# A chain of attention and feed-forward layers on one core: layer norm statistics taken pair by pair, and two norms merged

## What is computed

```python
def _layernorm(x, axis=-1, eps=1e-05):
    m = jnp.mean(x, axis=axis, keepdims=True)
    v = jnp.var(x, axis=axis, keepdims=True)
    return (x - m) / jnp.sqrt(v + eps)

x = x + _L0_xattn_ref(_layernorm(x), ctx_512, ...)            # cross attention, 16 heads, 1500 keys
x = x + _L0_ffn_ref(_layernorm(x), ...)                       # 8 experts, the best 2
x = x + _L1_xattn_ref(_layernorm(x), ctx_512, ...)
x = x + _L1_ffn_ref(_layernorm(x), L1_ffn_rhs)                # int8 product
x = x + _L2_xattn_ref(_layernorm(x), ctx_512, ctx_512, ...)
x = x + _L2_ffn_ref(_layernorm(x), ...)                       # product in the frequency domain
x = x + _L3_xattn_ref(_layernorm(x), ctx_512, ...)            # two attentions with MLPs
x = x + _L3_ffn_ref(_layernorm(x), ...)                       # routed blocks
```

```python
x = _ln(xx, ln1_g, ln1_b)
x = x + _mha(x, x, a1...)      # causal self attention, then MLP
x = _ln(x, ln2_g, ln2_b)
return x + _mha(x, ee, a2...)  # cross attention, then MLP
```

## Time and profile before

| | |
|---|---|
| median of 3 runs | 4266.44 us |
| profiled execution | 4266.73 us |
| its span | 4264.9 us |
| busy, share of the span: PE, DVE, ACT, POOL | 91%, 80%, 65%, 64% |
| L146 `bn_stats` | 224, median 0.276 us each |
| L149 `bn_aggr` | 224, median 0.149 us each |
| L155 subtract and multiply | 224, median 0.34 us each |
| L162 power, on POOL | 28, median 1.65 us each |

### The profile page before, as it was taken

How to read it: one execution, slowest core, us unless ns; L and a number is a source line. 1 busy time by engine, 2 the same in 40 slices (tenths; PEclk the granted TensorE clock), 3 DMA queues, 4 the chain that set the end, 5 groups by cost and what they waited for, 6 DMA issues and landing times. The chain is left out here.

```text
span 4264.9 us, 103800 instructions
## 1 busy us (share of the span) xinstructions
PE 3879.5 (91%) x40555; PEld 2833.5 (66%) x40555; DVE 3391.7 (80%) x6723; ACT 2768.2 (65%) x5364; POOL 2709.2 (64%) x2473
## 2 busy tenths in 40 slices
PE   6999999978887999999889999996897799999986
PEld 4777777755554777777657777775676477777765
DVE  7999998768778888888688888886754788888863
ACT  5777777644545777777567777773442577777752
POOL 3887888756764777777647676775000377767761
PEclk9999999979998999999889999998898799999988
DMA  4333333124432111111011111110000111111100
GB/s 113 96 90 96 89 95 96 32 63 131 122 109 69 47 44 50 44 50 47 10 49 52 42 47 46 48 47 20 3 1 17 44 50 44 50 44 47 47 17 15
DMA packets 112883, 236.97 MB, mean 56 GB/s; under 512 B 14984, under 2 KB 53016, under 8 KB 111016
## 3 DMA queue, kind: packets, MB, share of 16 engines
q1 hardware_dynamic: 111944, 230.27, 18.9%
q10 hardware_dynamic: 448, 0.06, 0.0%
HBM read 165.10 MB, written 50.26 MB: 50 GB/s over the span
## 5 line engine op out<-in xcount | busy, mean ns | idle before, releaser
L520 POOL TENSOR_TENSOR wst<-wst 125x384 bf16<-125x384 f32 (+1 forms) x1536 | 1635.3, 1065 | 801.3 <-ACT wst L724 735.0
L724 ACT ACTIVATE wst<-ps 125x448 f32<-125x448 f32 x3072 | 1499.0, 543 | 406.8 <-PE ps L166 397.6
L781 DVE TENSOR_TENSOR wst<-wst 125x512 bf16<-125x512 f32 (+1 forms) x1536 | 1395.7, 909 | 255.0 <-ACT wst L724 246.5
L166 PE MATMUL ps<-big,cx 128*125 128x448 bf16 (+1 forms) x6144 | 1436.3, 355 | 0.0
L166 PEld LDWEIGHTS ps<-cx,wst 125*128 125x128 bf16 x23040 | 1105.7, 98 | 355.4 <-issue 60.5
L166 PE MATMUL ps<-cx,wst 125*128 125x65 bf16 (+2 forms) x23040 | 1202.8, 204 | 28.4 <-POOL wst L520 14.3
L166 PEld LDWEIGHTS ps<-big,cx 128*125 128x125 bf16 (+1 forms) x6144 | 814.9, 137 | 271.6 <-ACT wst L724 8.9
L166 PE MATMUL ps<-cx,big 128*128 128x500 bf16 (+1 forms) x2688 | 714.0, 319 | 28.2 <-DVE wst L751 14.5
L748 DVE CUSTOM_DVE_ANT_0 wst<-ps,wst 128x500 bf16<-128x500 f32 x896 | 603.2, 673 | 162.2 <-PE ps L166 122.9
L673 ACT ACTIVATE wst<-ps 128x500 bf16<-128x500 f32 x896 | 531.0, 593 | 231.5 <-PE ps L166 187.6
L751 DVE TENSOR_REDUCE wst<-ps 128x1 f32<-128x500 f32 x896 | 600.0, 670 | 34.0 <-PE ps L166 26.7
(11 more groups left out here) (240 smaller groups left out, 4101.9 us busy)
## 6 DMA issues: line engine op xcount, KB each, us to landing
cx<-ctxT SPq DMA_DIRECT2D x96, 375.0 KB, 3.5
cx<-ctxN SPq DMA_DIRECT2D x64, 377.9 KB
cx<-in_ctxN SPq DMA_DIRECT2D x64, 375.0 KB
cx<-ctxT SPq DMA_DIRECT2D x96, 187.5 KB, 3.8
ctxN<-cx SPq DMA_DIRECT2D x32, 377.9 KB
ynN<-cx SPq DMA_DIRECT2D x32, 377.9 KB
cx<-ynN SPq DMA_DIRECT2D x32, 377.9 KB
cTs<-in_ctxT SPq DMA_DIRECT2D x64, 187.5 KB, 6.8
```

Of the source, the lines that this page charges most:

```text
L166: return t.matmul(o, l, r, start=start, stop=stop, skip_group_check=True)
L520: g.tensor_tensor(pl[r][0:KP, at:], pf[r][0:KP, at:], pf[r][0:KP, at:].bitcast(BF16)[:, 1::2], ALU.subtract).then_inc(s["plp"], 1)
L724: e.activation(pf[T % 3][0:KP, cols], bank(2 + n2 % 3, 448)[0:KP], ACT.Exp, scale=scale).then_inc(s["ev"], 1)
L781: v.tensor_tensor(pl[r][0:KP, 0:to], pf[r][0:KP, 0:to], pf[r][0:KP, 0:to].bitcast(BF16)[:, 1::2], ALU.subtract).then_inc(s["pl"], 1)
```

## The change

A norm's statistics become steps: step p takes `bn_stats` of pair p and `bn_aggr` of pair p - 1, and at p = 8 and p = 16 the addition of eps for a half. Of the norms behind the cross attentions (NEXT_NORM), the experts, the frequency layer, the causal attention and the MLPs, step p - 1 is issued behind the addition that finishes pair p, and the last two steps behind the loop. The norm behind the int8 product takes its steps group by group behind POOL's four additions. The two norms in a row become one, with the factor 1/sqrt((1 + eps) var + eps^2). So thirteen norms are left, numbered 0 to 12. POOL's power stands ahead of its stage wait and of the `memset`s of `oo`, `hid` and `hid4`. The wide additions of the MLPs move behind the transposes. The diff, cut where a hunk only renumbers or repeats:

```diff
+        def step_stats(n, p):
+            return 34 * n + 2 * p + (p > 8)
+
+        def dve_norm_step(v, w, n, src, p):
+            if p < NP:
+                v.bn_stats(st[:, p, :], src[:, p, :]).then_inc(s["bn"], 1)
+            if p:
+                w.wait_ge(s["bn"], max(34 * n + 1, step_stats(n, p - 1)))
+                v.bn_aggr(mv[:, p - 1, :], st[:, p - 1, :]).then_inc(s["bn"], 1)
+            if p in (8, 16):
+                cols = slice(p - 8, p)
+                w.wait_ge(s["bn"], 34 * n + (17 if p == 8 else 33))
+                if n == TWICE:
+                    v.tensor_scalar(ve[:, cols], mv[:, cols, 1], 1.0 + EPS, EPS * EPS, ALU.mult, ALU.add).then_inc(s["bn"], 1)
+                else:
+                    v.tensor_scalar(ve[:, cols], mv[:, cols, 1], EPS, None, ALU.add).then_inc(s["bn"], 1)
+
+        def dve_norm_apply(v, w, n, src, dst):
             for h in range(2):
                 w.wait_ge(s["pw"], 2 * n + h + 1)
                 for p in range(8 * h, 8 * h + 8):
                     v.tensor_scalar(dst[:, p, :], src[:, p, :], mv[:, p, 0:1], rs[:, p:p + 1],
                                     ALU.subtract, ALU.mult).then_inc(s["xn"], 1)

+        def dve_norm(v, w, n, src, dst):
+            for p in range(NP + 1):
+                dve_norm_step(v, w, n, src, p)
+            dve_norm_apply(v, w, n, src, dst)
...
-                w.wait_ge(s["bn"], 34 * n + 17 * h + 17)
+                w.wait_ge(s["bn"], 34 * n + 18 + 16 * h)
...
+        NEXT_NORM = (1, 3, 5, 11)
...
                     v.tensor_tensor(add_to[:, p, :], add_to[:, p, :], bank(7, 128), ALU.add).then_inc(s["ad"], 1)
+                    if p:
+                        dve_norm_step(v, w, NEXT_NORM[ci], add_to, p - 1)
+            w.wait_ge(s["ad"], NP * (ci + 1))
+            for p in (NP - 1, NP):
+                dve_norm_step(v, w, NEXT_NORM[ci], add_to, p)
...
         def pool_f0(g, w):
+            pool_norm(g, w, 1)
             wait_cross(w, 0)
             for i, o in enumerate(oo):
                 g.memset(o, 0.0).then_inc(s["clear"], 1)
                 w.wait_ge(s["clear"], i + 1)
-            pool_norm(g, w, 1)
...
         def dve_f0(v, w):
             wait_cross(w, 0)
-            dve_norm(v, w, 1, x, xn)
+            dve_norm_apply(v, w, 1, x, xn)
...
+                        if e == E - 1 and p:
+                            w.wait_ge(s["acc"], 16 + 4 * m + q)
+                            dve_norm_step(v, w, 2, x, p - 1)
...
         def dve_l1(v, w):
             wait_f0(w)
-            dve_norm(v, w, 2, x, xn)
+            for p in (NP - 1, NP):
+                dve_norm_step(v, w, 2, x, p)
+            dve_norm_apply(v, w, 2, x, xn)
...
         def dve_l2(v, w):
-            wait_f1(w)
-            dve_norm(v, w, 4, x, xn)
+            for p in range(NP + 1):
+                w.wait_ge(s["qx"], min(p, NP - 1) // 4 + 1)
+                dve_norm_step(v, w, 4, x, p)
+            dve_norm_apply(v, w, 4, x, xn)
...
                 v.tensor_tensor(x[:, p, :], x[:, p, :], bank((6 + p) % 8, 128), ALU.add).then_inc(s["dx"], 1)
+                if p:
+                    w.wait_ge(s["dx"], p)
+                    dve_norm_step(v, w, 6, x, p - 1)
...
         def pool_a1(g, w):
+            for n in (6, 7):
+                pool_norm(g, w, n)
             wait_f2(w)
-            for n in (6, 7, 8):
-                pool_norm(g, w, n)
...
         def dve_a1(v, w):
             wait_f2(w)
-            dve_norm(v, w, 6, x, xn)
+            for p in (NP - 1, NP):
+                dve_norm_step(v, w, 6, x, p)
+            dve_norm_apply(v, w, 6, x, Lx)
             w.wait_ge(s["xn"], 112)
-            dve_norm(v, w, 7, xn, Lx)
-            w.wait_ge(s["xn"], 128)
             w.wait_ge(s["w"], 544)
             dve_affine(v, w, Lx, gb[:, 0, :], gb[:, 1, :], 0)
-            dve_norm(v, w, 8, Lx, xn)
+            dve_norm(v, w, 7, Lx, xn)
...
                                        op0=ALU.mult, op1=ALU.add).then_inc(s["ax"], 1)
+                if p:
+                    w.wait_ge(s["ax"], p)
+                    dve_norm_step(v, w, 8, xn2, p - 1)
...
         def pool_mlp(g, w, i, norm):
+            pool_norm(g, w, norm)
+            if i:
+                wait_cross(w, 3)
+            else:
+                wait_a1(w)
             for c, h in enumerate(hid):
                 g.memset(h, 0.0).then_inc(s["clear"], 1)
                 w.wait_ge(s["clear"], CLEAR_MLP + 2 * i + c + 1)
-            pool_norm(g, w, norm)
...
         def dve_mlp(v, w, i, norm, src, dst, v0):
-            dve_norm(v, w, norm, src, xn)
+            dve_norm_apply(v, w, norm, src, xn)
             dve_turned_affine(v, w, (7, 9)[i], (xT, vec[:, v0:v0 + 1], vec[:, v0 + 1:v0 + 2]))
+            v.tensor_tensor(dst[:, :, :], dst[:, :, :], src[:, :, :], ALU.add).then_inc(s["xp"], 1)
             w.wait_ge(s["xp"], i + 1)
             for p in range(NP):
                 w.wait_ge(s["ho"], 16 * i + p + 1)
                 v.tensor_tensor(dst[:, p, :], dst[:, p, :], bank(p % 4, 128), ALU.add).then_inc(s["hd"], 1)
+                if p:
+                    w.wait_ge(s["hd"], 16 * i + p)
+                    dve_norm_step(v, w, norm + 1, dst, p - 1)
+            w.wait_ge(s["hd"], 16 * i + NP)
+            for p in (NP - 1, NP):
+                dve_norm_step(v, w, norm + 1, dst, p)
...
         def pool_f4(g, w):
+            pool_norm(g, w, 12)
             wait_mlp(w, 1)
...
-            pool_norm(g, w, 13)
```

More of the change, by code:

```diff
@@ L22 @@
 EPS = 1e-5
+TWICE = 6
 E, F = 8, 256
@@ L139, in build @@
             "lT_0", "lT_1", "lT_2", "lN_0", "lN_1", "lN_2", "lx_0", "lx_1", "plp", "half", "dif", "qd_0", "qd_1", "fh", "fl", "tops_0", "tops_1", "clear", "wl", "xsh", "xsl")}
-        def dve_norm(v, w, n, src, dst):
-            for h in range(2):
-                ps_, at = range(8 * h, 8 * h + 8), 34 * n + 17 * h
-                for p in ps_:
-                    v.bn_stats(st[:, p, :], src[:, p, :]).then_inc(s["bn"], 1)
-                w.wait_ge(s["bn"], at + 8)
-                for p in ps_:
-                    v.bn_aggr(mv[:, p, :], st[:, p, :]).then_inc(s["bn"], 1)
-                w.wait_ge(s["bn"], at + 16)
-                v.tensor_scalar(ve[:, 8 * h:8 * h + 8], mv[:, 8 * h:8 * h + 8, 1], EPS, None, ALU.add).then_inc(s["bn"], 1)
+        def step_stats(n, p):
[14 more added lines that the diff above has]
+        def dve_norm_apply(v, w, n, src, dst):
             for h in range(2):
@@ L1309, in pool_l1 @@
         def pool_l1(g, w):
+            pool_norm(g, w, 2)
             wait_f0(w)
@@ L1312, in pool_l1 @@
             w.wait_ge(s["cr"], 1)
-            pool_norm(g, w, 2)
         def pe_l1(t, w):
@@ L1391, in dve_f1 @@
             wait_cross(w, 1)
-            dve_norm(v, w, 3, x, xn)
+            dve_norm_apply(v, w, 3, x, xn)
             w.wait_ge(s["xn"], 64)
@@ L1489, in dve_f2 @@
             wait_cross(w, 2)
-            dve_norm(v, w, 5, x, xn)
+            dve_norm_apply(v, w, 5, x, xn)
             dve_turned(v, w, 5, xT)
@@ L1548, in pe_a1 @@
             wait_f2(w)
-            pe_turn(t, w, xn, s["xn"], 128, 1)
+            pe_turn(t, w, xn, s["xn"], 112, 1)
             pe_fold(t, w, 3, 128, 32, *pre_weights(32, 128), s["w"], 544)
@@ L1794, in pool_a2 @@
         def pool_a2(g, w):
-            pool_norm(g, w, 10)
             w.wait_ge(s["af"], 6)
@@ L1799, in pool_a2 @@
                 w.wait_ge(s["xa"], p + 1)
-            pool_norm(g, w, 11)
+            pool_norm(g, w, 10)
             for g4 in range(4):
@@ L1818, in pe_a2 @@
             r.then_inc(s["qbm"], 1)
-            pe_turn(t, w, xn, s["xn"], 176, 1)
+            pe_turn(t, w, xn, s["xn"], 160, 1)
             w.wait_ge(s["cr"], 3)
@@ L1827, in dve_a2 @@
             wait_mlp(w, 0)
-            dve_norm(v, w, 10, Lx, xn2)
-            w.wait_ge(s["xn"], 176)
+            dve_norm_apply(v, w, 9, Lx, xn2)
+            w.wait_ge(s["xn"], 160)
             dve_affine(v, w, xn2, gb[:, 4, :], gb[:, 5, :], 4)
-            dve_norm(v, w, 11, xn2, xn)
+            dve_norm(v, w, 10, xn2, xn)
             dve_turned_affine(v, w, 8, (xT, vec[:, 10:11], vec[:, 11:12]))
@@ L1905, in pe_f4 @@
             wait_mlp(w, 1)
-            pe_turn(t, w, xn, s["xn"], 208, 1)
+            pe_turn(t, w, xn, s["xn"], 192, 1)
             wait_turned(w, 6)
@@ L1953, in dve_f4 @@
             wait_mlp(w, 1)
-            dve_norm(v, w, 13, x, xn)
+            dve_norm_apply(v, w, 12, x, xn)
             dve_turned(v, w, 6, xT, 10)
@@ L2072, in _ @@
             wait_a1(w)
-            pe_mlp(t, w, 0, 144, rows4[1])
+            pe_mlp(t, w, 0, 128, rows4[1])
             pe_a2(t, w)
@@ L2076, in _ @@
             wait_cross(w, 3)
-            pe_mlp(t, w, 1, 192, rows4[3])
+            pe_mlp(t, w, 1, 176, rows4[3])
             pe_f4(t, w)
@@ L2095, in _ @@
             wait_a1(w)
-            v.tensor_tensor(Lx[:, :, :], Lx[:, :, :], xn2[:, :, :], ALU.add).then_inc(s["xp"], 1)
```

(18 more changed lines are left out.)

## The result

The changed kernel takes **4237.59 us** (median of 4 runs, 4234.72 to 4240.97) against 4264.25 of the kernel before on the same chip (median of 4, 4261.61 to 4266.81): a ratio of 0.9938 (95% interval 0.9925 to 0.9950), 26.7 us less. The forecast was 4242. The profiled execution took 4236.73, its span is 4234.9. One execution of all those reported here, in the last experiment, ran at a much lower granted clock (0.72 of full speed, 5049.55 us) and is left out of that experiment's figures.

What follows compares the result with a forecast made beforehand. PE waits at norms between the long loops, not inside the cross loops. Gains of 27.2 us, less 3.0 for the cross loops, plus 0.5 for the clock, give 24.7: 4266.7 to 4242 us, range 4230 to 4253.

Steps and rivals of the forecast that it cites:

- The head: From the last addition's end to a norm's first use: 4.89 us shrinks to 0.75, a gain of 4.14.
- Norms 5 and 9: Two norms whose shorter wait behind the last addition was to gain 4.1 us each.
- Norms 1, 3 and 4 hidden: Norms ahead of the experts and around the fold, covered by other work: gain 0; rival that they weren't, 4231, chance 0.04.
- The meeting with the clears: Subtractions beside POOL's memsets pass only at changes between them: done at 7.3 us instead of 4.2 in each MLP.
- the last layer: Norm 12: 12.7 us from last addition to last subtraction becomes 9.4, a gain of 3.3, bounds 2.5 and 7.8.
- The rival that the clears don't stop DVE: Subtractions pass POOL's memsets: 10 us more gain, 4232; chance 0.20, shared with PE's clock staying up.
- the one of dearer steps: Rival: alternating statistics and aggregates cost 0.43 us a step, 0.16 more for 41 on the path: 6.5 us, 4248; chance 0.14.
- Norm 2: Behind the experts: 3.2 us gained before the subtractions, 3.2 us lost to steps in the last four expert iterations; net 0.
- Cross loop 0: DVE has no idle time there, so 15 steps reach PE nearly whole: 2.5 us lost, bounds 0 and 6.
- Loops 1 to 3: Cross loops where DVE idles 0.49 us behind each addition, so a 0.27 step fits: 0.5 us lost for 45.
- Norms 6 and 7: Merged into one behind the frequency loop: gain 9.3 us, after 0.75 for steps and a wait for late loads.
- Clock: PE's granted clock may stay up after shorter waits: 0 to 3 us for each MLP, 0.5 taken in all.

Runs made afterwards that it cites:

- the last experiment: Changed kernel with clears, affine load, Q-half doubling, norm 2 steps and norm 10 powers moved, and POOL's 16 additions behind norm 10's last subtraction: 4211.64 us.
- both experiments on the clears: Changed kernel with MLP and last-layer clears behind the norm's last subtraction, 4225.86 us; changed kernel with only the MLPs' hid clears cut in eight pieces, 4230.90 us.
- one experiment: Changed kernel with POOL's clears in both MLPs and the last layer waiting until the norm's last subtraction: 4225.86 us, ratio 0.9911.

## Why the prediction was right, and where it wasn't

**Right, by its own steps.** The head: 0.79 us for 0.75. Norms 5 and 9: 4.3 and 4.1 for 4.1. Norms 1, 3 and 4 hidden: moving the steps of 1 and 3 back changed neither stretch, and the one from cross loop 1 to cross loop 2, in which 3 and 4 stand, kept its length (48.4 and 48.4 us before, 48.0 and 48.7 after). The meeting with the clears, read from the earlier trace rows: 6.9 to 7.2 us for 7.3 in the MLPs, 8.59 for 8.2 to 8.6 in the last layer, whose head and subtractions together gave the 3.3 that were forecast, and both experiments on the clears bear out that subtractions pass only at changes. The rival that the clears don't stop DVE is out (it was priced at 10 us with 3.7 for the last layer, where the forecast's own bounds, 7.8 - 3.3, give 4.5; without the meeting the subtractions took 4.4 less), and so is the one of dearer steps: steps of norm 7 in a row, waits included, start 0.26 us apart.

```profile
2977.18 0.26 DVE L148 BATCH_NORM_STATS2 st<-cx 128x6 f32<-128x128 f32 x1
2977.36 0.16 DVE L151 BATCH_NORM_AGGREGATE mv<-st 128x2 f32<-128x6 f32 x1
2977.44 0.26 DVE L148 BATCH_NORM_STATS2 st<-cx 128x6 f32<-128x128 f32 x1
```

**Norm 2, wrong.** The forecast had 3.2 us of steps cancelled by 3.2 us of shorter head. The steps were sized well (3.0 up to the end of POOL's last piece), but the head's gain wasn't one: it took the end of that stretch to be the norm's, where it was the loads'. The row that would have told it is PE's wait of 9.17 us for `big<-big` at 1310.96, in the trace of before all along. In the four profiles of the table the stretch lost 4.7 us: 3.0 up to the end of POOL's last piece, 1.7 between the first load and the first product. Over the eight changed profiles with these steps and this order the second part is 0.8 (13.8 and 14.9 before, 15.2 in the mean after) and scatters from 14.5 to 16.2, so the loss is 4.0, of which 3.0 is shown to be the steps'.

**Cross loop 0, mis-sized.** The forecast took 2.5 us for 15 steps since DVE had no idle time there (15 x 0.17; its own row leaves 0.27 - 0.06 = 0.21 a step). They cost 0.2 in all. Busy isn't the same as without slack: 0.39 us of the split behind most additions was waiting for POOL. Loops 1 to 3 cost nothing either and got some 3 us shorter where 0.5 of loss was forecast; their slack was 0.27 + 0.6, more than the 0.49 of idle time. So the cross loops came out 5 to 6 us better than forecast and norm 2 4 to 5 worse: that these nearly cancel, and that the total fits, is luck.

**Norms 6 and 7, a little short.** 8.7 for 9.3. The step in the frequency loop cost 0.34 instead of 0.75, but the wait for the loads was 4.22 instead of 3: the forecast counted to the end of the traffic, and the semaphore comes some 2 us behind it.

**Clock.** 0.5 was taken for the MLPs. In the first MLP head and subtractions gave 3.3 and 3.5 us, for 3.2 forecast; the rest of the 4.3 is the clock, with the first eight products at 5.84 and 4.74 us, where they took 6.13 and 6.29 before and up to 6.31 in other changed kernels. It showed elsewhere too: 2.5 us ahead of cross loop 3 in most kernels, and up to 2.5 in the router's products (5.46 and 7.00 before, 6.98 after, 4.45 in one experiment). Which level a stretch gets after such a change couldn't be told, and the runs don't settle it.

**Two pages.** Each subtraction above that met a clear, and each split that met POOL's, lasted until its end or beyond. So the engines don't meet in semaphores alone. The Trainium skill (SBUF — State Buffer, Who interferes with whom) says that DVE in a two-port mode and GpSimd exclude each other for a whole instruction, and that a DVE instruction with two SBUF inputs contends only with a GpSimd instruction that reads SBUF. The trace agrees with both as far as it goes (in which mode the subtractions ran, no row shows): the subtractions waited for clears, the split, whose two inputs lie in SBUF, for POOL's split, and the wide addition of two SBUF inputs took 2.29 beside a clear. The prediction had held this last row against the shorter wording of another page. Of the halves that landed behind two sets of loads, the Trainium skill (DMA: Bandwidth & Descriptors, Queues, rings and completion order) says that each DMA engine consumes its descriptors in ring order; 8.5 us instead of 14.5 to 16.2 with only the order of issue changed agrees with it. That the copies merely shared bandwidth with the loads isn't excluded by that run.

## What to carry to other kernels

When a step moves out of a head, look up what the first consumer waits for last: if it's a DMA, the head wasn't the price, and whatever is put into the loop that feeds that DMA's store is paid in full. A busy engine can have slack: compare an instruction's duration where it meets the other engine's work with its shortest. And where POOL and DVE must meet, keep POOL's instructions short or behind DVE's; of the single edits tried here, moving three groups of clears gained most (15 us between the medians, 12 in the stretches that hold them).
